# Attention blocks on one core: score tiles issued in pairs, projections in two halves, outputs of eight heads in one block, 64-row score matmuls, 48-row stack reads

## The reference, cut to what matters

```python
def _L1_conv_ref(x, t, gn_scale, gn_bias, w_qkv, b_qkv, w_out, b_out):
    xn = group_norm(x, gn_scale, gn_bias)
    qkv = xn.reshape(b, hs * ws, c) @ w_qkv + b_qkv
    q, k, v = jnp.split(qkv.reshape(b, hs * ws, NUM_HEADS, 3 * HEAD_DIM), 3, axis=-1)
    q = q / jnp.sqrt(jnp.float32(HEAD_DIM))
    ...
    attn = jax.nn.softmax(jnp.einsum('bhqd,bhkd->bhqk', q, k), axis=-1)
    out = jnp.einsum('bhqk,bhkd->bhqd', attn, v)
    h = out.transpose(0, 2, 1, 3).reshape(b, hs * ws, 128) @ w_out + b_out
    return xn + h.reshape(b, hs, ws, c)
```

## Time and profile before

| what | value |
|---|---|
| median of three runs | 2756.16 us (2754.94 to 2777.43) |
| the profiled execution's own time | 2752.47 us |
| its span, first to last instruction | 2750.4 us |
| TensorE matmul busy | 2525.4 us (92%), 12332 records |
| VectorE busy | 1729.6 us (63%) |
| ScalarE busy | 1537.7 us (56%) |
| mean granted TensorE clock | 0.909 |

### The profile page before, as it was taken

One profiled execution on the slowest core, in us unless ns is written; L12 is line 12 of the kernel. 1 busy time (PEld: TensorE's weight loads), 2 busy tenths in 40 slices (PEclk: granted clock), 3 DMA queues, 4 the chain that ended last, 5 costly groups with the idle time before them and its releaser, 6 DMA issues.

```text
span 2750.4 us, 32645 instructions
## 1 busy us (share of the span) xinstructions
PE 2525.4 (92%) x12332; PEld 1163.4 (42%) x12332; DVE 1729.6 (63%) x3245; ACT 1537.7 (56%) x2009; POOL 226.8 (8%) x182
## 2 busy tenths in 40 slices
PE   4899899999999998999989999899998999999999
PEld 2333233333353335533354334543345433543666
DVE  2687566777858775676656766567665774554332
ACT  2266544665647664476644765357643776357554
POOL 3001010101000100001000010101000010000000
PEclk7589865888999999999999989998999999999999
DMA  7301340314040402204040040401304022000000
GB/s 142 47 1 26 60 70 8 64 22 78 1 77 10 72 6 41 45 9 78 1 77 16 3 78 8 70 17 30 49 16 66 5 38 41 1 9 1 5 5 16
DMA packets 53482, 96.81 MB, mean 35 GB/s; under 512 B 6736, under 2 KB 9424, under 8 KB 53200
## 3 DMA queue, kind: packets, MB, share of 16 engines
q1 hardware_dynamic: 53328, 94.74, 19.5%
HBM read 55.91 MB, written 37.75 MB: 34 GB/s over the span
## 4 chain that ended last, share of the span: by engine, by line
PE 76%; DVE 16%; ACT 3%; issue 3%; DMA 2%; SPq 1%; POOL 0%; ACTq 0%; DVEq 0%
PE outs L1126 18%; PE work L1081 15%; PE pairs L1103 9%; DVE part_max L907 9%; PE pairs L1139 9%; PE outs L1157 9%; PE work L1013 5%; PE work L1057 4%; PE work L1062 2%; DVE neg_max L931 2%; PE work L1053 2%; ACT probs L785 2%; PE outs L1166 1%; DVE o_turn L917 1%; DVE stats L838 1%
## 5 line engine op out<-in xcount | busy, mean ns | idle before, releaser
L907 DVE TENSOR_REDUCE part_max<-work 128x1 f32<-128x512 f32 x2048 | 1302.9, 681 | 579.1 <-PE work L1081 577.0
L785 ACT ACTIVATE probs<-pairs 128x1024 f32<-128x1024 f32 x1024 | 1005.0, 1023 | 386.4 <-PE pairs L1103 350.4
L1081 PE MATMUL work<-k_stack,q_stack 48*128 48x512 f32 x2048 | 748.2, 505 | 97.6 <-DVE part_max L907 68.9
L1103 PE MATMUL pairs<-q_stack,k_stack 50*128 50x512 f32 x2048 | 608.8, 480 | 32.8 <-ACT probs L785 23.5
L1081 PEld LDWEIGHTS work<-k_stack,q_stack 48*128 48x128 f32 x2048 | 323.2, 204 | 741.1 <-DVE part_max L907 350.7
L1126 PE MATMUL outs<-probs,v_heads 128*32 128x512 f32 x4096 | 611.9, 673 | 0.0
L1103 PEld LDWEIGHTS pairs<-q_stack,k_stack 50*128 50x128 f32 x2048 | 262.4, 202 | 205.9 <-ACT probs L785 119.4
L791 ACT ACTIVATE probs<-pairs,neg_max 128x1024 f32<-128x1024 f32 x128 | 142.7, 1115 | 346.0 <-DVE neg_max L931 346.0
L931 DVE TENSOR_REDUCE neg_max<-pairs 128x1 f32<-128x1024 f32 x128 | 156.7, 1224 | 175.0 <-PE pairs L1139 175.0
L1139 PE MATMUL pairs<-k_full,q_full 128*128 128x512 f32 x512 | 261.1, 634 | 0.0
L1157 PE MATMUL outs<-probs,v_full 128*128 128x256 f32 x1024 | 243.7, 392 | 0.7 <-DVE y L952 0.7
...
## 6 DMA issues: line engine op xcount, KB each, us to landing
...
k_scratch<-parts SPq DMA_DIRECT2D x32, 512.0 KB, 2.8
q_scratch<-parts SPq DMA_DIRECT2D x32, 512.0 KB, 13.0
q_stack<-shift_parts SPq DMA_DIRECT2D x256, 4.0 KB
tmp<-x SPq DMA_DIRECT2D x7, 512.0 KB, 3.4
...
```

Of the source, the lines that this page charges most:

```text
L785: nc.scalar.activation(probs[:, plan.prob[u], 2 * n:2 * n + 2, :], pairs[:, n, :, :], ACT.Exp, scale=HEAD_SCALE).then_inc(exp_done, 1)
L907: nc.vector.tensor_reduce(part_max[:, r % 2, column:column + 1], bank_of(("tile", r, n)), AX_X, ALU.max, negate=True).then_inc(tile_max, 1)
L1081: nc.tensor.matmul(bank_of(("tile", r, n)), qs[rows, i, a, heads, P * t:P * (t + 1)], ks[rows, i, keys, heads, :], start=True, stop=True). ...
L1103: last = nc.tensor.matmul(pairs[:, n, half, :], ks[rows, i, key // QT, first + n, P * (key % QT):P * (key % QT + 1)], qs[rows, i, a, first ...
```

## The change

- Tiles are handed out in pairs, one of each row half (`PAIRS`, `tile_pairs`, `FIRST_PAIRS` 20). A head beat takes one pair between its two `pair` items and the rest behind `values`.
- The first chunk of a head beat that has TensorE work now stands between the tiles and the second `pair` item. Projections of layers 2 and 3, of the later images of layer 0 and of the last of layer 1 go in two halves over two beats: a `piece` with the first 256 columns and a `chunk` with the rest, in one bank that is held from one to the other. Places of several chunks move; the projections of image 1 go from ahead of the first tiles into beats 1 to 6.
- At the end of a full stretch two beats' `pair` items stand in the last accumulation.
- Outputs: GpSimd writes the scaled 16 channels of two rounds side by side into `o_both`, VectorE transposes back once per two rounds, `oT` is half as large, and an out chunk multiplies once by a weight block merged at the start (`merge`, four DMAs). `back` stands for half of the rounds.
- Score matmuls use 62 rows (tiles) and 64 rows (pairs); q rows 48 to 61 of each half are zero, the shift rows are 62 and 63.
- The scratch in DRAM holds the three blocks of 16 rows, so a write is three DMAs of 256 KB and a read two of 48 rows and 768 KB; `STACK_SLOTS` is 11.

The diff, cut to its core:

```diff
-    FIRST_TILES = 40
+    FIRST_PAIRS = 20
...
+    def chain(self, beat, layer, image, names, step=1):
         for n in names:
             for m in n.split("+"):
-                self.put(beat, ("chunk", m, layer, image))
-            beat += 1
+                if step == 2:
+                    self.put(beat, ("piece", m, layer, image))
+                self.put(beat + step - 1, ("chunk", m, layer, image))
+            beat += step
...
+            if i == 1:
+                self.project(h(0, 1), 0, i, one)
             if i >= 2:
-                before = g0 - 2
-                at = h(before, {2: 16, 3: 21, 4: 21}.get(i, 10))
+                at = h(g0 - 2, {2: 16, 3: 23, 4: 18}.get(i, 14))
                 put(at - 3, ("load", i))
-                self.chain(at, 0, i, ["in0", "in1", *NORM])
-                self.project(h(g0 - 1, 1), 0, i, one)
-            put(h(g0, 28), ("chunk", "out0", 0, i))
-            put(h(g0 + 1, 4), ("chunk", "out1", 0, i))
-            late = i == 0 or i == IMAGES - 1
-            self.chain(h(g0 + 1, 5 if late else 7), 1, i, NORM)
+                at = self.chain(at, 0, i, ["in0", "in1", "stats", "gn1", "gn2"])
+                self.chain(at + (1 if i == 4 else 0), 0, i, ["apply"])
+                self.project(h(g0 - 1, 1), 0, i, one, 1 if i < 4 else 2)
+            self.chain(h(g0, 28), 0, i, ["out0"])
+            self.chain(h(g0 + 1, 4), 0, i, ["out1"])
...
-    STACK_SLOTS = 15
+        at = {b: pairs[counts[b]:counts[b + 1]] for b in range(ends)}
+        at[-1] = pairs[:self.FIRST_PAIRS]
+        return at
+    STACK_SLOTS = 11
...
+        order = [("load", 0), ("constants",), ("load", 1), ("merge",)]
         for i in range(2):
             order += [("chunk", n, 0, i) for n in ("in0", "in1", *NORM)]
-            for n in PROJECTIONS:
-                order.append(("chunk", n, 0, i))
-                if n in SPLIT:
-                    order.append(("write", i, SPLIT.index(n)))
-                if n in ("k1", "q1"):
-                    order.append(("read", i, n[0]))
             if i == 0:
+                for n in PROJECTIONS:
+                    order.append(("chunk", n, 0, i))
+                    if n in SPLIT:
+                        order.append(("write", i, SPLIT.index(n)))
+                    if n in ("k1", "q1"):
+                        order.append(("read", i, n[0]))
                 order.append(("biases",))
-        return order + self.with_shift(-1)
-    def with_shift(self, b):
-        order = []
+        return order + sum(self.tile_pairs(-1), [])
...
+    def tile_pairs(self, b):
+        groups = []
         for r, n in self.tiles.get(b, []):
-            order.append(("tile", r, n))
-            if n == 2 and r > 0 and ("shift", r - 1) not in self.shifted:
-                order.append(("shift", r - 1))
-                self.shifted.add(order[-1])
+            groups.append([("tile", r, 2 * n), ("tile", r, 2 * n + 1)])
+            if n == 1 and r > 0 and ("shift", r - 1) not in self.shifted:
+                groups[-1].append(("shift", r - 1))
+                self.shifted.add(groups[-1][-1])
         for r, n in self.tiles.get(b - 1, [])[-1:]:
-            if n == TILES - 1 and ("shift", r) not in self.shifted:
-                order.append(("shift", r))
-                self.shifted.add(order[-1])
-        return order
+            if n == PAIRS - 1 and ("shift", r) not in self.shifted:
+                groups[:1] = [(groups[0] if groups else []) + [("shift", r)]]
+                self.shifted.add(("shift", r))
+        return groups
...
+        groups, extra = self.tile_pairs(b), self.extra.get(b, [])
+        kinds = [self.beats[a][0] if 0 <= a < len(self.beats) else None for a in range(b - 2, b + 3)]
+        def take(count):
+            taken = sum(groups[:count], [])
+            del groups[:count]
+            return taken
         if kind == "head":
             r, s = n // KT, n % KT
-            order = [] if before == "full" else [("pair", 2 * n)]
-            order += tiles[0:2]
-            if before != "full":
+            first, second = kinds[1] == "full", kinds[0] == "full" and kinds[1] == "head"
+            own = not first and not second
+            order = [("pair", 2 * n)] if own else []
+            order += take(1)
+            middle = [e for e in extra if self.on_tensor_engine(e)][:1]
+            order += middle
+            if own:
                 order.append(("pair", 2 * n + 1))
-            if before == "full":
+            if first:
                 order.append(("proj", self.beats[b - 1][1] // 2))
             elif n > 0:
                 order.append(("values", n - 1))
                 if s == 0:
                     order.append(("outputs", r - 1))
-            if s == 3 and r > 0 and not self.follows_full(n - 3):
+            if s == 3 and r % 4 in (3, 0) and r > 0 and not self.follows_full(n - 3):
                 order.append(("back", r - 1))
-            order += tiles[2:] + extra
-            if after[0] == "full":
-                m = after[1]
-                order += [("scores", m), ("values", n), ("outputs", r), ("scores", m + 1), ("back", r)]
+            order += take(len(groups)) + [e for e in extra if e not in middle]
+            if kinds[3] == "full":
+                m = self.beats[b + 1][1]
+                order += [("scores", m), ("values", n), ("outputs", r), ("scores", m + 1)]
+                groups.extend(self.tile_pairs(b + 1))
+                order += take(len(groups) - 1) + [("back", r)] + take(1)
             return order
-        last = after[0] != "full"
-        near = last or b + 2 >= len(self.beats) or self.beats[b + 2][0] != "full"
-        order = [("turn", n, 0), ("turn", n, 1), *tiles[0:1]]
-        if not near:
+        if kinds[1] == "head":
+            groups = []
+        order = [("turn", n, 0), ("turn", n, 1)]
+        m = n // 2
+        if n % 2 and kinds[0] == "full":
+            order.append(("proj", m - 1))
+        order += take(1)
+        if kinds[4] == "full":
             order.append(("scores", n + 2))
-        elif b + 2 < len(self.beats):
-            u = after[1] if last else self.beats[b + 2][1]
-            order.append(("pair", 2 * u + (1 if last else 0)))
-        order += tiles[1:3]
-        m = n // 2
-        if n % 2 == 0 and before == "full":
+        elif "head" in kinds[3:]:
+            u = self.beats[b + (1 if kinds[3] == "head" else 2)][1]
+            order.append(("pair", 2 * u + (1 if kinds[3] == "head" else 0)))
+        order += take(1)
+        if n % 2 == 0 and kinds[1] == "full":
             order += [("pv", m - 1, k) for k in range(KT)]
-        elif n % 2 and self.beats[b - 2][0] == "full":
-            order.insert(2, ("proj", m - 1))
-        order += tiles[3:] + extra
-        if last and after[0] is not None:
-            order += self.full_end(n, False)
+        order += take(len(groups)) + extra
+        if kinds[3] == "head":
+            u = self.beats[b + 2][1]
+            order += [("pv", m, k) for k in range(QT)] + [("pair", 2 * u)]
+            order += [("pv", m, k) for k in range(QT, KT)] + [("pair", 2 * u + 1)]
         return order
+    def on_tensor_engine(self, item):
...
-            if kind in ("tile", "turn", "shift") or kind == "chunk" and item[1] not in NO_BANK:
+            if kind == "chunk" and ("piece", *item[1:]) in self.bank:
+                self.bank[item] = self.bank["piece", *item[1:]]
+                half_done.remove(self.bank[item])
+            elif kind in ("tile", "turn", "shift", "piece") or kind == "chunk" and item[1] not in NO_BANK:
+                while n % WORK_BANKS in half_done:
+                    n += 1
                 bank = n % WORK_BANKS
                 n += 1
+                if kind == "piece":
+                    half_done.add(bank)
                 self.bank[item], self.before[item] = bank, held.get(bank)
-                held[bank] = item
+                held[bank] = ("chunk", *item[1:]) if kind == "piece" else item
...
+        o_both = sb("o_both", [P, 2, HALF // 32, 32])
+        oT = sb("oT", [P, TOKENS])
...
-        scratch = {n: nc.dram_tensor(f"{n}_scratch", [PARTS, 2 * HEADS, HD, HALF], F32, kind="Internal").ap()
+        scratch = {n: nc.dram_tensor(f"{n}_scratch", [len(Q_PART), HD, 2, HEADS, HALF], F32, kind="Internal").ap()
                    for n in "qk"}
...
-                        sp.wait_ge(stacked[n], 96 * g)
-                    to = scratch[n][:, HEADS * half:HEADS * (half + 1), :, :]
-                    sp.dma_start(to.rearrange("j h r t -> (h r) j t"), parts[:, at, :, :].bitcast(F32)
-                                 ).then_inc(parts_out[at], 16)
+                        sp.wait_ge(stacked[n], 32 * g)
+                    for b, part in enumerate(K_PART if n == "k" else Q_PART):
+                        to = scratch[n][b, :, half, :, :].rearrange("r h t -> h r t")
```

(56 more changed lines are left out.)

119 lines of the change are left out of this document (62 added, 57 removed).

## The result

| what | before | changed |
|---|---|---|
| median, measured side by side | 2765.49 us | 2849.98 us (2843.42 to 2851.55) |
| ratio, 95% interval | | 1.038 (1.032 to 1.044) |
| profiled execution, its span | 2752.47, 2750.4 us | 2851.16, 2849.0 us |
| mean granted clock | 0.909 | 0.946 |
| TensorE at 1.2 GHz (sum over the clock records) | 499 us | 309 us |

A forecast was written before the change was run, and what follows sets the result against it. TensorE was taken as the bound, busy 92% of the span and partly at 1.2 GHz. The terms summed to -22 us, from 2752.5 to 2730.5, with 3 us for the median 2733 us; range 2632 to 2825.

The forecast's parts named there:

- 64 rows: Score matmuls: no change in time per matmul, but less time at the low clock, -105 us (bounds 0 and -150).
- Tiles in pairs: Head beats: three-tile beats become two- and four-tile ones, whose bank wait outweighs the saved steps, +83 us.
- Outputs: Out chunks and transposes back: two matmuls in place of four, -27 us, and half the VectorE transposes, -15 us.
- Full beats: Full beats: fewer lone tiles and idle tails, -47 us; score matmuls moved into the stretches' last accumulation, -10 us.
- Projections in the middle, in two halves: Head beats with projections: split runs and held banks, late halves +72 us, early items +35; bounds +0 to +150.
- 48-row stacks: Stack reads and writes: faster reads, tiles begin 11 slots behind the last q chunk, smaller stage gaps, -11 us.
- start: Kernel's start: first tiles wait for the stack read, image 1's projections move into beats, -5 + 8 = +3 us.
- ScalarE idles while a whole chunk runs, and a half leaves it fed: Projection beats: argument for the faster rival (halves free, clock up everywhere), 2601 us, believed to 2667; chance 0.24.
- The clock: TensorE's granted clock: long low-clock stretches half to all gone, slices 2 to 7 at 8 or more, -105 us.
- Eight heads' outputs: Out chunks: two matmuls in place of four, 64 records fewer at 0.43 us on TensorE's path, -27 us.
- The port rule: Stack reads: rate goes by ports reached, 48 rows reach eight of sixteen; an estimated two thirds of today's time.
- Stacks come late: Slower rival, q and k stacks: writes take twice as long, 14 stages short by up to 5 us, +70, 2803 us; 0.07.

The follow-up runs named there:

- b_rows64: Kernel before with only the 62 and 64 rows in the score matmuls: 2683.48 us, ratio 0.970.
- wl_old_dma: Changed kernel with whole projections, chunks behind values and tiles, and the scratch, writes and reads of the kernel before: 2615.27 us, ratio 0.944.
- a_old_dma: Changed kernel with the scratch, writes and reads of the kernel before: 2820.20 us, ratio 1.020.
- swl_old_dma: Changed kernel with single tiles, whole projections behind the tiles, and the scratch, writes and reads of the kernel before: 2636.78 us, ratio 0.953.
- old_plan: Changed kernel with the order of work of the kernel before (single tiles, whole chunks behind the values, image 1 ahead): 2686.69 us, ratio 0.974.
- old_plan_pairs: Changed kernel with the order of work of the kernel before, but tiles handed out in pairs: 2689.95 us, ratio 0.974.

## Why the prediction was wrong, point by point

Its terms beside what the runs give for them, one after the other from before to changed:

| step | predicted | measured | between |
|---|---|---|---|
| *64 rows* (clock) | -105 | -82 | before (2765.5), b_rows64 (2683.5) |
| *Tiles in pairs*, *Outputs*, *Full beats* | +83 - 42 - 57 = -16 | -68 | b_rows64, wl_old_dma (2615.3) |
| *Projections in the middle, in two halves*, late and early | +107 | +205 | wl_old_dma, a_old_dma (2820.2) |
| *48-row stacks*, start | -8 | +30 | a_old_dma, changed (2850.0) |
| sum | -22 | +85 | |

With the new transfers the third row is 163 and the fourth 72, so these two are not independent. The second row also holds the moved chunks, the 11 slots and image 1's projections in beats 1 to 6, which the prediction counted under *48-row stacks* and start.

**The step that failed is *Projections in the middle, in two halves*.** Its sign was right, its size, 163 to 205, lay above the upper bound of 150 by either path. The prices of the new beats were right: a half on two tiles 2.72 (predicted 2.7), on four tiles 3.95 and 4.37 (4.2), a whole chunk in the middle 3.15 and 4.38 (3.15 and 4.45). Two other factors of the product were wrong. The first is what the halves were set against: 1.26 for a whole late chunk, which is its price in the three-tile beat of the kernel before. The pairs abolish that beat, and on two and four tiles a late chunk costs 1.06 and 0.60, 0.83 on average; over 100 chunks that is an estimated 43 us more to lose. (The same chunks make the +83 of *Tiles in pairs* too large: 2.93 + 1.26 was reckoned where 3.54 is measured.) The second is the count: 299 items stand in the middle by this kernel's order, not some 240. The halves among them are 191 (some 200 predicted), but 108 are whole chunks of any kind, where 40 were priced at 35 us; at 0.19 and 0.84 us, with a third of them on two tiles, they come to an estimated 68. So 107 + 43 + 33 = 183, between the two paths. The rival in which halves are free, "ScalarE idles while a whole chunk runs, and a half leaves it fed", had it backwards: ScalarE's idle time for a `pair` is 336 us with late whole chunks, 395 with late halves, 426 with whole ones in the middle and 491 in the changed kernel.

By the path with the new transfers this term is 56 us short and the stacks' -8 is 80 short, so that a second step failed beside it: the transfers, whose sign was wrong (below).

**The clock.** Right in direction: slices 2 to 7 are at 7 to 9 tenths where the kernel before had 5 to 9, and rows filled with zeros do it, without a cost per matmul that shows. The only cost found is at the start, below. The size, -105 against -82, took credit for the wrong part. With 48 rows the kernel before has 499 us at 1.2 GHz, the old order with the new engines' side 530 and the changed order 698: the new order lost clock, some 168 us of it, an estimated 50 us at 0.3, which the rows had to win back too. That the spread halves are the reason isn't shown: with 64 rows there is less low clock with them (309 us against 322 in the middle, 272 against 308 behind the values).

***Tiles in pairs*, +83.** Refuted as a loss: +3 in the old order, -21 beside the old transfers (swl_old_dma to wl_old_dma, whose executions overlap), -43 in the changed order. The four-tile beat is 2.94 us (predicted 2.93) and the two-tile beat 1.90 (1.94); but the three-tile beat that they were set against is 2.14 only undisturbed. Over the 111 plain ones at 1.00 in old_plan the mean is 2.30, since 18 of them took 2.4 to 4.7, most of it waits for maxima and for ScalarE. From old_plan to old_plan_pairs the plain beats lose 25 us (666 to 691) and the full stretches give 18 back (755 to 737): that is the measured size of the -47 for pairs in *Full beats*; the -10 for their ends was not isolated.

***Eight heads' outputs*, -27.** The term is there: the out chunks' matmuls are busy 65.6 us in b_rows64 and 37.7 in old_plan, and a three-tile beat with an out chunk takes 4.24 and 3.38 us, which over 32 chunks is an estimated 27 us. It did not show in old_plan's time, where the new transfers stand too: the first `pair` is at 112.7 us instead of 98.5, and 302 us are at 1.2 GHz instead of 270.

***48-row stacks*, -11 and start, +3.** The sign was wrong. The first tile starts 12 us later than before (73.1 us, before 61.0), the first `pair` 7 us later (99.9, before 92.9). Chain of waits of the changed kernel at the start, below one line of the same chain before:

```profile
9.35 6.88 DVE q_stack L1006
...
22.64 3.77 PE work L1091 x4
...
32.49 6.42 DMA k_scratch<-parts
...
39.70 12.76 DMA k_stack<-k_scratch
```
```profile
17.22 3.76 PE work L1057 x4
```

Five of the 12 us are there before the first write: VectorE fills half of the zero rows (L1006, 6.88 us) ahead of the first image's statistics, so the first projection starts at 22.64 instead of 17.22. The prediction had this hidden by the DMA at the start. The first write then takes 6.42 us, where it took 2.74.

The read of 1.5 MB is inside the 12 to 15 us of the bounds. The port rule of the Trainium skill ("SBUF — State Buffer", section "Door 1: The DMA port swizzle") gave an estimated two thirds of today's time; 12.76 us against 11.6 to 14.4 from the earlier trace rows is no such gain. The writes are where the other rule bears. DMA share in tenths and GB/s in 40 slices, 20 to 36 us of before and 28 to 60 us of the changed kernel:

```profile
DMA  0000000899569970004999997999989999999999
GB/s 0 0 0 0 0 0 0 333 379 389 210 241 384 389 297 0 0 0 92 230 266 123 92 133 113 154 97 123 108 97 159 128 97 102 118 128 154 92 113 108
```
```profile
DMA  0445554555553002799999999999865555555410
GB/s 23 41 131 195 184 141 113 187 202 202 195 200 141 13 0 59 246 187 120 138 131 105 192 205 123 131 143 120 151 202 202 205 205 202 202 205 205 174 72 8
```

Writes alone ran at 9 tenths and 389 GB/s; now they run at 5 tenths and 205. That is half of the engines, as the Trainium skill has it in "DMA: Bandwidth & Descriptors", section "Why a DMA increments its semaphore by 16 and not by 1": the new write's outer size is 8 heads. The trace agrees in busy share and in rate; which engines ran it does not say. The rival *Stacks come late* had the mechanism (writes that take longer) and nearly the late order's price (70; 72), but not the place: no list of waits behind the start has a tile waiting for a stack; it is the start, the image's load, the shift's rows and the clock.
